# Row stretch of a cross-attention kernel: both heads' banks used in neighbouring pairs, with one maximum and one exponential over each pair, and another order of the prologue

## The reference, cut to what matters

```python
q = (x @ Wq + bq).reshape(b, lq, H, D)        # 256 queries a batch, H = 16, D = 64
k = (embeds @ Wk + bk).reshape(b, lk, H, D)   # 1601 keys a batch
v = (embeds @ Wv + bv).reshape(b, lk, H, D)
scores = jnp.einsum('bqhd,bkhd->bhqk', q, k) * SCALE
attn = jax.nn.softmax(scores, axis=-1)
ctx = jnp.einsum('bhqk,bkhd->bqhd', attn, v).reshape(b, lq, AD)
return ctx @ Wo + bo
```

## Time and profile before

| | us |
|---|---|
| median of 3 runs | 2730.99 (2728.54 to 2731.56) |
| the profiled execution's own time | 2729.38 |
| its span in the profile | 2727.6 |
| TensorE busy | 2659.0 (97% of the span) |
| VectorE busy | 2122.0 (78%) |
| GpSimd busy | 2152.3 (79%) |
| ScalarE busy | 1723.4 (63%) |
| mean granted clock of TensorE | 0.989 of 2.4 GHz |

### The profile page before, as it was taken

One profiled execution on the slowest core, in us unless ns is written; L12 is line 12 of the kernel. 1 busy time (PEld: TensorE's weight loads), 2 busy tenths in 40 slices (PEclk: granted clock), 3 DMA queues, 4 the chain that ended last, 5 costly groups with the idle time before them and its releaser, 6 DMA issues.

```text
span 2727.6 us, 67860 instructions
## 1 busy us (share of the span) xinstructions
PE 2659.0 (97%) x26920; PEld 2280.4 (84%) x26920; DVE 2122.0 (78%) x4293; ACT 1723.4 (63%) x3470; POOL 2152.3 (79%) x1749
## 2 busy tenths in 40 slices
PE   5999999999999999999999999999999999999977
PEld 5888888888888888888888888888888888888855
DVE  6687878788787887878778787878878788787744
ACT  3666676666666666756657666666666666666632
POOL 1778888888788877888878888888888787888845
PEclk7999999999999999999999999999999999999988
DMA  4000000000000000000000000000000000000030
GB/s 101 7 22 7 27 10 9 24 8 27 9 8 25 11 23 10 21 12 11 26 7 22 11 25 11 8 24 9 25 9 23 10 10 23 8 11 9 12 99 27
DMA packets 81086, 53.28 MB, mean 20 GB/s; under 512 B 14239, under 2 KB 78453, under 8 KB 80768
## 3 DMA queue, kind: packets, MB, share of 16 engines
q1 hardware_dynamic: 75600, 45.27, 5.9%
q0 software_dynamic: 2048, 3.66, 0.4%
q10 hardware_dynamic: 3120, 0.01, 0.1%
HBM read 40.76 MB, written 8.72 MB: 18 GB/s over the span
## 4 chain that ended last, share of the span: by engine, by line
PE 95%; DVE 2%; POOL 1%; issue 1%; ACT 1%; DMA 0%; SPq 0%; POOLq 0%; DVEq 0%; ACTq 0%
PE ps L1484 26%; PE ps L1452 22%; PE ps L1448 10%; PE ps L1439 5%; PE ps L1430 4%; PE ps L1432 4%; PE ps L1431 4%; PE ps L1409 3%; PE ps L1411 3%; PE ps L1410 3%; PE ps L1500 3%; PE ps L1524 2%; PE ps L1385 1%; POOL out_dram L694 1%; PE ps L1367 1%
## 5 line engine op out<-in xcount | busy, mean ns | idle before, releaser
L622 POOL TENSOR_TENSOR key_sums<-key_sums,prob_T 65x512 f32<-65x512 f32 x1402 | 1816.2, 1295 | 161.7 <-POOL key_sums L622 2.2
L1048 DVE TENSOR_REDUCE mx<-ps 128x1 f32<-128x400 f32 (+1 forms) x2048 | 1055.9, 569 | 249.5 <-PE ps L1439 208.5
L818 ACT ACTIVATE prob_T<-ps 128x512 f32<-128x512 f32 x1536 | 832.8, 596 | 92.8 <-PE ps L1452 54.3
L1484 PE MATMUL ps<-prob_T,v_sb 128*64 128x256 f32 (+1 forms) x6656 | 740.5, 379 | 0.8 <-ACT prob_T L818 0.8
L1452 PE MATMUL ps<-q_hi,k_hi 64*128 64x256 f32 (+1 forms) x3328 | 734.8, 278 | 1.4 <-ACT prob_T L818 1.4
L1452 PE MATMUL ps<-q_lo,k_hi 64*128 64x256 f32 (+1 forms) x3328 | 732.8, 277 | 0.0
L1452 PE MATMUL ps<-q_hi,k_lo 64*128 64x256 f32 (+1 forms) x3328 | 731.6, 277 | 0.0
L1484 PEld LDWEIGHTS ps<-prob_T,v_sb 128*64 128x64 f32 (+1 forms) x6656 | 478.2, 137 | 241.4 <-ACT prob_T L818 1.7
L1452 PEld LDWEIGHTS ps<-q_hi,k_hi 64*128 64x128 f32 (+1 forms) x3328 | 578.0, 180 | 7.4 <-ACT prob_T L818 6.7
L1439 PE MATMUL ps<-k_hi,q_hi 64*128 64x400 f32 (+1 forms) x2048 | 580.4, 351 | 1.2 <-DVE q_lo L1039 1.2
L1448 PE MATMUL ps<-shift,shift_w 64*128 64x512 f32 (+1 forms) x1792 | 562.0, 381 | 2.7 <-ACT shift L789 1.4
(11 more groups left out here) (198 smaller groups left out, 3580.1 us busy)
## 6 DMA issues: line engine op xcount, KB each, us to landing
shift_f<-row_shifts SPq DMA_DIRECT2D x256, 64.0 KB, 2.6
ctx_raw<-in_ctx_dram SPq DMA_DIRECT2D x16, 768.0 KB
row_shifts<-nm_T SPq DMA_DIRECT2D x512, 0.5 KB
prob_T<-in_L_ffn_W_dram SPq DMA_DIRECT2D x12, 256.0 KB, 5.1
slots_in<-no_row SPq DMA_DIRECT2D x1, 2080.0 KB, 14.3
v_sb<-slots_in SPq DMA_DIRECT2D x8, 260.0 KB, 5.8
x_in<-in_x_dram SPq DMA_DIRECT2D x8, 256.0 KB, 2.9
out_dram<-x1s SPq DMA_DIRECT2D x16, 128.0 KB, 4.0
```

The costliest lines, as they stand in the source:

```text
L622: op = nc.gpsimd.tensor_tensor(acc[0:rows, :, :], acc[0:rows, :, :], prob_T[0:rows, :, k, :], ALU.add)
L818: nc.scalar.activation(prob_T[:, h, 2 * i - 2:2 * i, :].rearrange("p k t -> p (k t)"), ps[:, bank, :], ACT.Exp).then_inc(ring_act, 1)
L1048: v.tensor_reduce(mx[:, qt, h, c:c + 1], ps[:, at.bank("mx", r, c, qt, h), 0:WID[c]], AX.X, ALU.max).then_inc(ring_dve, 1)
L1484: last = mm(ps[h * DH:h * DH + DH, bank, 0:T], v_sb[0:rows, r % NJ // 2 % 2, k, v0 + h * DH:v0 + h * DH + DH], prob_T[0:rows, h, k, :], st ...
```

## The change

- **Order of the ring and of TensorE.** In each unit the two maxima come first, then both heads' shifts, then the score matmuls of head 0 and head 1 in turn, both at the same step. The two banks of a pair stand at neighbouring places of the ring, the first at an even place; where the count is odd, one place is left empty (60 of 5430 in all).
- **One wait for a pair.** Both score banks are asked for before the first shift matmul.
- **One read for a pair.** ScalarE takes one exponential over both banks (2 x 512 columns), VectorE one maximum over both (2 x 400). Each frees two places when it ends.
- **Prologue.** GpSimd makes the fourth ternary matrix and clears the tables; TensorE turns weights and x ahead of the context; ScalarE copies out all of `w_T`; the first value fills move ahead of `step_x1`, the maxima behind them; `wv_lo` moves ahead on GpSimd, `wq_lo` back on VectorE, and two of the four `keys_low` ahead of `residual`.

```diff
+        if len(fills) % 2:
+            fills.append((None, None))
+        for h in range(2):
+            put(owner, *key, h)
...
             for i, unit in enumerate(MAX_UNITS):
+                if following:
+                    heads_pair("dve", "mx", r + 1, *unit)
                 if i < UNITS:
-                    put("act", "s", r, i, 0)
-                if following:
-                    maximum(r + 1, unit, 1)
-                if i < UNITS:
-                    put("act", "s", r, i, 1)
-                if following:
-                    maximum(r + 1, unit, 0)
+                    heads_pair("act", "s", r, i)
...
                 for h in range(2):
                     act.wait_ge(rows_full[h], at.full("s", s, i, h))
-                    bank = at.bank("s", s, i, h)
-                    if i > 0:
-                        nc.scalar.activation(prob_T[:, h, 2 * i - 2:2 * i, :].rearrange("p k t -> p (k t)"),
-                                             ps[:, bank, :], ACT.Exp).then_inc(ring_act, 1)
...
+                bank = at.bank("s", s, i, 0)
+                if i > 0:
+                    nc.scalar.activation(prob_T[:, :, 2 * i - 2:2 * i, :].rearrange("p h k t -> p h (k t)"),
+                                         ps[:, bank:bank + 2, :], ACT.Exp).then_inc(ring_act, 2)
...
-                    for h in (1, 0):
+                    for h in range(2):
                         dve.wait_ge(rows_full[h], at.full("mx", r, c, qt, h))
-                        v.tensor_reduce(mx[:, qt, h, c:c + 1], ps[:, at.bank("mx", r, c, qt, h), 0:WID[c]],
-                                        AX.X, ALU.max).then_inc(ring_dve, 1)
+                    bank = at.bank("mx", r, c, qt, 0)
+                    v.tensor_reduce(mx[:, qt, :, c], ps[:, bank:bank + 2, 0:WID[c]], AX.X, ALU.max)\
+                        .then_inc(ring_dve, 2)
...
-                first, = banks_of(at, ("s", s, i, 0), also=[("k", s, 3), ("q", s)] if i == 0 else [])
+                if unit:
+                    for h in range(2):
+                        maximum(at, s + 1, *unit, h)
+
+                banks = banks_of(at, ("s", s, i, 0), ("s", s, i, 1), also=[("k", s, 3), ("q", s)] if i == 0 else [])
...
+                for part in steps:
+                    last = [score_step(s, h, banks[h], *part) for h in range(2)]
+                for h in range(2):
+                    last[h].then_inc(rows_full[h], 1)
...
+            pool.wait_ge(tern_in, 16 * 6)
+            pool.wait_ge(thresholds, 1)
+            own(nc.gpsimd.tensor_scalar(w_tmp[:, 3, :], w_rows[:, 3, :], w_half[:, 3:4], None, ALU.is_gt))
...
             at = start
+            turn_weights()
+            step_tokens(at, 0)
             for c in range(4):
                 context(at, 0, c)
-            turn_weights()
-            step_tokens(at, 0)
-            pe.wait_ge(setup_ev_act, 1)
-            pe.wait_ge(setup_ev_dve, 1)
+            pe.wait_ge(setup_ev_act, 2)
             step_rkv(at, 0)
             step_products(at, 0)
             context_read(at, 0)
             pe.wait_ge(wk_split, 1)
             for c in range(4):
                 keys(at, 0, c)
+            pe.wait_ge(wv_split, 1)
+            for n in range(V_FILLS):
+                values(at, 0, n)
             step_x1(at, 0)
```

More of the change, by code:

```diff
@@ L77, in all_fills, with heads_pair @@
     step = lambda i, *names: [put(STEP_OWNERS[name], name, i) for name in names]
-    def maximum(r, unit, h):
-        put("dve", "mx", r, *unit, h)
+    def heads_pair(owner, *key):
+        if len(fills) % 2:
+            fills.append((None, None))
+        for h in range(2):
+            put(owner, *key, h)
+    step(0, "xt")
     for c in range(4):
         put("dve", "ctx", 0, c)
-    step(0, "xt", "r", "kk", "vv", "o", "ss")
+    step(0, "r", "kk", "vv", "o", "ss")
     for c in range(4):
         put("dve", "k", 0, c)
+    for n in range(V_FILLS):
+        put("act", "v", 0, n)
     step(0, "x1t")
@@ L89, in all_fills @@
     for unit in MAX_UNITS:
-        maximum(0, unit, 1)
-        maximum(0, unit, 0)
-    for n in range(V_FILLS):
-        put("act", "v", 0, n)
+        heads_pair("dve", "mx", 0, *unit)
     for c in range(4):
@@ L184, in held_by @@
         place = self.find(*key) - len(RING)
+        while place >= 0 and self.ring.fills[place][1] is None:
+            place -= len(RING)
         return [place] if place >= 0 else []
@@ L866, in _ @@
             at = start
+            act.wait_ge(setup_tr, 1)
+            copy(w_T[:, 0:3, :], ps[:, 7, 0:3 * P].rearrange("p (m n) -> p m n", m=3)).then_inc(setup_ev_act, 1)
+            nc.scalar.activation(w_T[:, 3, :], ps[:, 7, 3 * P:4 * P], ACT.Copy, scale=lnw_c[:, :]).then_inc(setup_ev_act, 1)
+            tokens_in(at, 0)
             for c in range(4):
                 context_high(at, 0, c)
-            act.wait_ge(setup_tr, 1)
-            copy(w_T[:, 0:3, :], ps[:, 7, 0:3 * P].rearrange("p (m n) -> p m n", m=3)).then_inc(setup_ev_act, 1)
-            tokens_in(at, 0)
-            gate_and_keys(at, 0)
             act.wait_ge(wv_in, 16)
             copy(wv_hi[:, :], wv_rows).then_inc(w_hi, 1)
+            gate_and_keys(at, 0)
             act.wait_ge(wq_in, 16)
@@ L881, in _ @@
                 keys_high(at, 0, c)
+            for n in range(V_FILLS):
+                values_out(at, 0, n)
             x1T_out(at, 0)
@@ L884, in _ @@
             queries_high(at, 0)
-            for n in range(V_FILLS):
-                values_out(at, 0, n)
             for c in range(4):
@@ L1245, in _ @@
             gated(at, 0)
+            mean_square(at, 0)
+            dve.wait_ge(biases_in, 16 * 3)
+            v.tensor_scalar(bq_s[:, :], bq_c[:, :], SCALE, None, ALU.mult).then_inc(wq_split, 1)
+            for c in range(2):
+                keys_low(at, 0, c)
+            residual(at, 0)
+            step_moments(0)
+            for c in range(2, 4):
+                keys_low(at, 0, c)
+            normed(0)
             dve.wait_ge(wq_in, 16)
@@ L1340, in turn_weights @@
             def turn_weights():
-                pe.wait_ge(tern_ready, 4)
+                pe.wait_ge(tern_ready, 3)
+                pe.wait_ge(tern_out, 1)
                 for m in range(4):
@@ L1563, in batch @@
                         elif following:
-                            maximum(at, s + 1, *unit, 1)
-                            maximum(at, s + 1, *unit, 0)
+                            for h in range(2):
+                                maximum(at, s + 1, *unit, h)
                     if part == (1, 5):
@@ L1616, in _ @@
             for unit in MAX_UNITS:
-                maximum(at, 0, *unit, 1)
-                maximum(at, 0, *unit, 0)
-            pe.wait_ge(wv_split, 1)
-            for n in range(V_FILLS):
-                values(at, 0, n)
+                for h in range(2):
+                    maximum(at, 0, *unit, h)
             for c in range(4):
```

75 lines of the change are left out of this document (32 added, 43 removed).

## The result

| | before | changed |
|---|---|---|
| median, us | 2730.68 (2728.54 to 2731.56, 4 runs) | 2786.07 (2785.75 to 2787.11, 4 runs) |
| ratio, 95% interval | | 1.0206 (1.0193 to 1.0219) |
| span in the profile, us | 2727.6 | 2783.9 |

What follows compares the result with a forecast made beforehand. TensorE was taken to bound the kernel. Span 2729.38 plus 43.0 for waits in the row slots, less 3 in the prologue, gave 2769.4, stated as 2770 us; the 8-in-10 range was 2727 to 2790.

Steps and rivals of the forecast that it cites:

- Bound and mechanism: Row stretch: TensorE bounds, and units 3 and 5 wait 0.16 each for ScalarE's joint read, 0.32 us a slot.
- The loop: Row stretch, first shift through joint read to the next shift on that bank: 1.23 + 1.04 + 0.05 + 0.10 = 2.42, against 2.25.
- the tail: End of the row stretch, last unit's 0.94 plus 0.27 for the eighth maxima and the step to the values.
- Slots that start late: Seven slots with ScalarE's first copy late lose 0.9 each, 6.3; seven with VectorE's first maximum late lose 0.52 each, 3.6.
- The first slot of a batch: 14 slots whose units already wait; a joint read adds 0.1 each, 1.4 in all.
- Joint reads as such: Row stretch: joint exponential takes 1.04 and saves nothing alone; joint maximum takes 1.0, zero except where VectorE comes late.
- The order in step: TensorE's row stretch: both heads at the same step move no column and cost zero; a unit still streams 1.12.
- the one wait for two banks: Row stretch, main term: both banks come free together and are wanted at head 0's time; 99 slots x 0.32 = 31.7.
- Prologue: Before the first row stretch: first product near 17.0, 3 us off at the first shift, from 4.5 to 1.5.
- A: Rival for the row stretch: no wait appears, loop 2.25 or less; 2732 us, chance 0.14.
- B: Rival, faster: loop below 2.25 and head 1's trailing step had cost 0.05 a slot; 2721 us, chance 0.14.
- C: Rival, worse: row stretch loop of 2.48 and no gain in the prologue; 2789 us, chance 0.10.

Runs made afterwards that it cites:

- e4: Changed kernel with joint exponentials of all slots after the first reading only 384 of 512 columns of each bank: 2725.04 us, 1.0015 of the kernel before.
- e7: Changed kernel with joint exponentials of all slots after the first reading only 448 of 512 columns of each bank: 2760.52 us, 1.0112 of the kernel before.
- e9: Kernel before, with its TensorE order, own waits and single maxima, given only the joint exponential and the changed prologue: 2860.02 us, ratio 1.0478.
- e6: Changed kernel, but ScalarE waits for head 1's count alone before a joint exponential: 2778.92 us, 1.0180 of the kernel before.
- e10: Changed kernel with one maximum for each head again: 2786.94 us, 1.0210 of the kernel before.
- e3: Changed kernel with two exponentials a unit, each freeing its own bank, and each head's shift waiting for its own bank: 2758.57 us, ratio 1.0140.
- e12: Kernel before with the changed prologue, wk_lo held back until VectorE has made its three ternary matrices: 2724.63 us, ratio 0.9982.
- e8: Kernel before with the changed prologue, wk_lo held back until VectorE has made its three ternary matrices: 2725.51 us, ratio 0.9985.
- e1: Kernel before with only the changed prologue; ring, score units, exponentials and maxima as before: 2717.09 us, ratio 0.9989.
- e11: Kernel before with only the changed prologue, run again on another chip: 2726.95 us, ratio 0.9989.
- e2: Changed kernel with two exponentials a unit, each freeing its own bank, both banks still asked for before the first shift: 2770.92 us, ratio 1.0183.

## Why the prediction was right, and where its sizes were off

- **Bound and mechanism: right.** TensorE bounds, and it waits for ScalarE's reads in a loop that is longer than two units, and units 3 and 5 pay. e4 and e7 show the loop by its length, e9 that the joint read alone, on the order of before, is more than enough.
- **The loop: 2.42 taken, 2.44 and 2.47 measured.** It is 1.26 to the read at unit 1 and 1.29 at unit 3 (its shift counted from when it streams) where I took 1.23, a read of 1.03 where I took 1.04, 0.05 and 0.10 as taken. Part of the under-count is that the joint read waits for two counts: e6 gave 0.02 to 0.03 of it back a loop; the rest stays open. With the unit at 1.13 and the tail at 1.24 (1.12 and 1.21 taken) the slot loses 0.43 instead of 0.32. This is the term that was mis-sized: 99 slots x 0.11 = 11 us. (2 to 4 us of them are rounding in the working itself: unit 6 at 6.90 is 0.34 to 0.36 over 0.94 + 5 units, not 0.32.) With 6 from the slots that start late and 2.6 from single waits of 0.3 here and there, less 1.4 in the prologue and 1.6 between the row stretches, these are the 16 between forecast and result. It lies inside the bounds that I gave, 0.2 to 0.45, near the upper.
- **Slots that start late.** ScalarE late: 0.80 each (8.72 after 7.92), 0.9 taken. VectorE late: 0.88 (8.66 after 7.78), 0.52 taken, since the first joint maximum starts 1.2 into the slot and not 0.94, and unit 2 at 2.53. The first slot of a batch: 0.54 to 0.57 in six batches and 0.11 to 0.44 in the other nine, 5.3 in all, 0.1 each taken. Together these come to 7 x 0.80 + 7 x 0.88 + 5.3 = 17 where 11 was taken.
- **Joint reads as such: right.** 1.03 and 0.99 us, and the joint maximum worth nothing (e10).
- **The order in step: put at zero, and that holds for streaming alone** (e4, 7.81 after 7.79). The working charged all of the loss to the one wait for two banks. e3 shows 0.28 of the 0.43 with own waits and own reads: once the heads end together, ScalarE's second read ends 2.3 us after the shift, and its bank is wanted after 2.25. The sum doesn't suffer, since its loop was counted with the heads in step, but the cause was named too narrowly.
- **Prologue: 3 off taken, 4.4 off measured** at the end of the first row stretch, 6.1 at its first shift (55.96 after 62.07). The first product came at 18.04, not 17.0, for the 2.31 us step beside wk_lo; the fourth matrix on GpSimd, steps of 0.45 to 0.68, was ready at 10.7 and not late. The value fills took 4.6 us at full clock in the gap ahead of `step_x1` and held nothing up: they ended at 37.6, and `x_rows` was made by 37.5. The first slot gives back 1.7, as it takes 9.44 from its first shift to its end, after 7.73. Its shift comes by DMA and is cast by 55.8, three us after the first maxima, now that no value fills stand between them. TensorE was busy for 0.1 of the 2.8 us before 56.0, and its granted clock was 0.50 (1.2 GHz) from 56.7 to 60.0, where in the kernel before it was 1.00 throughout this stretch.
- **Rivals.** A and B fell: no middle slot is without waits. C was nearest in size (2789, for 2786), but by a loop of 2.48 with no gain in the prologue; in fact the loop was 2.45, the prologue gave more, and the odd slots made up the difference.
- **The advice to vectorize PSUM access** (the Trainium skill, "TensorEngine Tiling (Array Packing)", PSUM Bottleneck) reads in full "Vectorize PSUM access across multiple tiles in same bank"; the prediction left the last three words out. Done here over two banks, it gave the readers 61 us less on ScalarE and 81 on VectorE, and the kernel got 55 us slower, as neither was the bound. No run here shows it within one bank.
- **The version that the runs point to:** the row stretch of before with the new prologue, and wk_lo held back, 0.9982 (0.9973 to 0.9991) and 0.9985 (0.9976 to 0.9994) of the kernel before, some 4 to 5 us. e12 and e8 are the same program; its gain over the new prologue alone isn't settled.

Open: why the first slot of a batch is 0.6 to 0.8 us longer on some chips and not on one. The rows before it are alike in e1 and e11. In slot 32 of e11 TensorE's rows stand where they stand in e1 up to 3.9 us into the slot, yet both ScalarE's exponential of unit 2 and VectorE's maximum beside it start late, at 3.63 and 3.62 after 3.02 and 3.13. Both wait for head 0's count, so it is TensorE's count that comes late, and not a reader; what holds it isn't known. Whether the joint read pays with more room in the ring (three pairs of score banks and one of maxima) wasn't tried.

## What to carry to other kernels

Before two reads of a ring are joined, write down the loop of one buffer: filled from its first write, seen as full, read, seen as free, refilled. A joint read takes the later end of one buffer and the earlier need of the other into that same loop, so it costs although the reader becomes less busy; the slack to look at is that of the buffer needed first and not the mean. Keep a stagger between two producers if the reader works one after the other: the second read needs that time, and giving it up was 0.28 of the 0.43 us a slot here.

## What the runs showed of the hardware

- A weight load that has to wait for the bank of its matmul isn't hidden: 0.10 us behind the start of the shift (0.50 for 0.40), and the listed wait leaves that out. In e7 almost no wait is listed and 0.1 a loop is lost.
- One more semaphore wait in front of an instruction of ScalarE cost 0.02 to 0.03 us on the path (medians of 1.28 and 1.26 from unit 1's shift to the read, with two counts and with one). In e2, where the read waits for head 0's count alone, it is 1.19, but the read is another there.
- Two row halves of the array drift apart by themselves if only one of them waits (e3: 0.08 at unit 3, 0.20 at unit 4, 0.23 at unit 6), while the half that doesn't wait keeps 1.11 and 1.12 a unit up to unit 5.
- A VectorE step of 0.35 us took 2.31, and in e8 a scan of 0.69 took 2.56. Both started 0.2 to 0.4 us after a GpSimd operation of 2.4 us and ended within 0.6 us behind it; both read two operands from SBUF. A copy of 0.29, with one operand in SBUF, took 2.44 in e12 in the same way. A `kv` step that reads PSUM and SBUF, beside wv_lo, kept its 0.69. The Trainium skill ("SBUF — State Buffer", SBUF: two separate sides) says that a GpSimd operation and a VectorE operation in a two-port performance mode, or with two SBUF inputs, take one shared pair of ports, whole instruction by whole instruction. The two steps with two inputs agree; that the copy ran in such a mode no row here shows. The prediction, which put the turns at 12, left this out.
